# Writing the corner weights ahead of the wait for the transposes, and four value buffers for two, in a deformable convolution's sampling loop

## The chip, the cores and the metric

The kernel runs on one core of one Trainium2 chip (trn2). The metric is the device time of one execution in microseconds. TensorE multiplies and transposes, VectorE and ScalarE work element by element, GpSimd issues the gathers, SyncE issues the plain transfers. Engines run their own instruction streams and meet at semaphores only.

## The reference

Four blocks act on an activation of 8 images of 64 channels and 32x32 pixels, one after the other: attention with a wavelet split, two "adder" convolutions (sums of absolute differences), a quantized pair of 3x3 convolutions, and a residual block with a deformable convolution. The change lies in the last one. Cut to what matters:

```python
h = relu(bn(conv2d(x, rb_w1) + rb_b1, rb_bn1))
h = relu(bn(conv2d(h, rb_w2) + rb_b2, rb_bn2) + x)
off_out = conv2d(h, off_w) + off_b           # 54 maps: 2 groups x 9 taps x (y, x, mask)
py, px = offsets + pixel + tap               # per group, tap, pixel
val = sum over 4 corners of h[corner] * corner weight        # bilinear, zero outside
out = einsum('odck,bdckhw->bohw', dc_w, val * sigmoid(mask)) + dc_b
h = leaky_relu(bn(out, bn1), 0.1)
return x + leaky_relu(bn(conv2d(h, cv2_w), bn2), 0.1)
```

## The kernel before

Two images lie on the 128 partitions at a time (64 channels each), so the eight images are four pairs; "image" below means such a pair, b = 0 to 3. Everything of the earlier blocks is done when the phase `sampler` is at work on its steps.

For each image a chain of seven stages (`stage_pe`, `stage_act`, `stage_dve`, numbered 0 to 6) does the quantized block's convolutions, the two residual convolutions and the offset convolution (nine taps each, into PSUM banks 6 and 7), stores the pixels' channel rows to a table in device memory (each entry holds the four corner pixels of a position), and works out the gather indices `IDX` and the corner weights `W4` (masked, bilinear). For image 0 they run ahead of all steps.

Then an image has 16 steps (`STEPS`), 64 in all: a step `th` is 128 pixels of one of the two images that lie together. Its work is:

1. GpSimd: 18 indirect DMAs, one for each group and tap (line 1902), each fetching 128 table rows of 512 bytes into `G[th % 4]`. It waits for `used`, so a gather buffer is refilled only after its step's reduce, four steps back. These 18 are called a batch below.
2. ScalarE, `weigh(th)` (line 2054): copies the step's 18 x 4 corner weights from `W4` to the single buffer `WP` in PSUM bank 5.
3. VectorE (lines 1951 to 1961): waits for the gathers and the weights, multiplies in place (128 x 2304), reduces over the four corners into `VAL[:, th % 2]`, and frees the gather buffer. In the kernel before it waits ahead of the reduce until the transposes of step th-2 have read that value buffer.
4. TensorE (lines 2003 to 2023): five transposes of the values into PSUM, then, when ScalarE has copied them out, ten matmuls (five products in float32, each sent as two passes) with the kernel weights `DC`. Each is sent with a weight load of its own; the transposes too.
5. ScalarE (lines 2033 to 2047): the copy from PSUM to `VT`, in two instructions.

Eight steps fill a PSUM bank. Then ScalarE copies it to `Y`, VectorE applies the leaky ReLU, TensorE makes the 1x1 convolution (E below), ScalarE copies it to `U`, and VectorE does the last leaky ReLU and the addition (`finish`, lines 1963, 2025, 2056). VectorE's `finish` stands behind the first step of the next bank and waits for all of this.

The order on every engine is written out by `steps` (line 1873): sample step th, at every eighth step `finish` for the bank before, then one stage of the next image. TensorE does stage s behind step s of the 16, ScalarE and VectorE behind step s + 1 (`lag`). So image b + 1 is prepared between the first eight steps of image b; the last image's steps have nothing between them.

T52 and MM52 below are the transposes and the products of step 52.

Of the kernel before, what the change touches and what calls it, by code (L numbers as in the profile page):

```python
# [17 lines left out]
NB = B // HALVES  # L18
# [16 lines left out]
CG = CH // DG  # L35
# [3 lines left out]
STEPS = TILES * HALVES  # L39
GK = DG * TAPS  # L40
# [147 lines left out]
def program(nc, A, C, out):  # L188
# [3 lines left out]
    with outer:  # L192
# [1443 lines left out]
        def sampler(st, sb, sem):  # L1636
# [4 lines left out]


            STAGES = 7
            RING = 4
            ws = ("rb_w1", "rb_w2", "off_w")
            G = [sb(f"G{i}", [128, GK, 4 * CG]) for i in range(RING)]
            VAL = sb("VAL", [128, 2, GK, CG])
            VT = sb("VT", [128, 2, 5, 128])
            Y = sb("Y", [128, 2, BANK])
            U = sb("U", [128, 2, BANK])  # L1650
# [10 lines left out]
                   for i in range(3)]  # L1661
# [15 lines left out]

            arrived = [sem(f"arrived{i}") for i in range(RING)]
            used, val, t_ps, t_sb, d_ps, d_sb, leaky, e_ps, e_sb, final, written = (
                sem(n) for n in ("used", "val", "t_ps", "t_sb", "d_ps", "d_sb", "leaky", "e_ps", "e_sb", "final",  # L1680
                                 "written"))
            valued, weighed = (sem(n) for n in ("valued", "weighed"))
            WP = PS[:, 5, 0:GK * 4]
            off3 = OT[:, :, :].rearrange("p t (h c) -> p (t h) c", h=HALVES)
            PRE = PS[:, 6:8, :]
# [202 lines left out]
            with nc.Block() as blk:  # L1888
# [59 lines left out]
                def _(v):  # L1948
                    def sample(th):
                        gt = G[th % RING]  # L1950
                        v.wait_ge(arrived[th % RING], 16 * GK * (th // RING + 1))
                        v.wait_ge(weighed, th + 1)
                        g3 = gt[:, :, :].rearrange("p k (q c) -> p (k q) c", q=4)
                        v.tensor_tensor(g3, g3, WP.unsqueeze(2).broadcast_to([128, GK * 4, CG]), ALU.mult)  # L1954
                        v.drain()
                        if th >= 2:
                            v.wait_ge(t_ps, th - 1)
                        v.tensor_reduce(VAL[:, th % 2, :, :], gt[:, :, :].rearrange("p k (q c) -> p k c q", q=4),  # L1958
                                        AX.X, ALU.add)
                        v.drain().then_inc(val, 1)  # L1960
                        v.sem_inc(used, 1)
# [39 lines left out]
                @blk.tensor  # L2001
                def _(t):
                    def sample(th):
                        tl, h, k = th // 2, th % 2, th // per_bank
                        t.wait_ge(val, th + 1)
                        if th >= 2:
                            t.wait_ge(t_sb, th - 1)
                        flat = VAL[:, th % 2, :, :].rearrange("p k c -> p (k c)")
                        for c in range(5):
                            n = min(128, GK * CG - 128 * c)  # L2010
                            o = 128 * c if c < 4 else 128 * (th % 2)
                            mm = t.transpose(PS[0:n, th % 2 if c < 4 else 2, o:o + 128],  # L2012
                                             flat[:, 128 * c:128 * c + n], K["ident"][:, :])
                        mm.then_inc(t_ps, 1)
                        t.wait_ge(t_sb, th + 1)
                        if th % per_bank == 0 and k >= 2:
                            t.wait_ge(e_sb, k - 1)
                        for c in range(5):
                            n = min(128, GK * CG - 128 * c)
                            mm = t.matmul(PS[64 * h:64 * h + 64, 3 + k % 2, 128 * (tl % 4):128 * (tl % 4) + 128],  # L2020
                                          DC[0:n, c, :], VT[0:n, th % 2, c, :], start=(c == 0), stop=(c == 4))
                        if th % per_bank == per_bank - 1:
                            mm.then_inc(d_ps, 1)

                    def finish(k):
                        t.wait_ge(leaky, k + 1)
                        t.matmul(bank(3 + k % 2), CV2[:, 0, :], Y[:, k % 2, :], start=True, stop=True)\  # L2027
                            .then_inc(e_ps, 1)
                    steps(t, stage_pe, weights_pe, sample, finish, 0)

                @blk.scalar
                def _(a):
                    def sample(th):
                        k = th // per_bank
                        if th == 0:
                            weigh(0)
                        a.wait_ge(t_ps, th + 1)
                        a.activation(VT[:, th % 2, 0:4, :], PS[:, th % 2, :].rearrange("p (a c) -> p a c", c=128),  # L2038
                                     ACT.Copy)
                        a.activation(VT[0:64, th % 2, 4, :], PS[0:64, 2, 128 * (th % 2):128 * (th % 2) + 128], ACT.Copy)  # L2040
                        a.drain().then_inc(t_sb, 1)  # L2041
                        if th + 1 < NB * STEPS:
                            weigh(th + 1)
                        if th % per_bank == per_bank - 1:
                            a.wait_ge(d_ps, k + 1)
                            a.activation(Y[:, k % 2, :], bank(3 + k % 2), ACT.Identity, scale=INV[:, 2:3],  # L2046
                                         bias=SHIFT[:, 2:3]).then_inc(d_sb, 1)
# [42 lines left out]
```

## Time and profile before

| | |
|---|---|
| median of 3 runs | 4685.74 us (4657.04 to 4686.9) |
| the profiled execution | 4699.3 us, its span 4697.5 us |
| TensorE busy | 3017.8 us (64% of the span) |
| VectorE busy | 2951.6 us (63%) |
| ScalarE busy | 2245.1 us (48%) |
| GpSimd busy | 1156.9 us (25%) |
| packets of the gathers' queue | 36864, 75.57 MB |

Busy time is the time in which an engine executes; waiting for a semaphore isn't in it. In a timeline a row is: start, duration, engine, line of the kernel, operation, what it writes and reads, the count merged, and in brackets how long the engine was idle before it and which engine's event ended that ("issue": nothing that the profile shows; "remote": an event the profile can't place). "PE" is TensorE, "DVE" VectorE, "ACT" ScalarE, "POOL" GpSimd. A matmul's record tells when it was sent to the array and its modelled length; when its result was ready is seen from who waited for it. The two passes of a float32 product have a record each.

### The profile page before, as it was taken

How to read it: one execution, taken by the hardware profiler on the slowest of the kernel's cores; microseconds unless marked ns; L12 is line 12 of the kernel's file. 1: busy time of each engine (PE TensorE's matmuls, PEld its weight loads, DVE VectorE, ACT ScalarE, POOL GpSimd, SP SyncE). 2: the span in 40 equal slices, each digit the busy share in tenths (PEclk: the TensorE clock that was granted, in tenths of full speed). 3: DMA queues.
4: the chain of work that ended last, by engine and by line, in shares of the span. 5: the costliest groups of instructions: out<-in, count | busy, mean ns of one | idle time of the engine just before them, and what ended most of it. 6: DMA issues, size and time to landing. Idle time of an engine off the chain costs nothing. (4 is left out here: it accounts for less than half of the span.)

```text
span 4697.5 us, 54006 instructions
## 1 busy us (share of the span) xinstructions
PE 3017.8 (64%) x20519; PEld 1314.3 (28%) x20519; DVE 2951.6 (63%) x3460; ACT 2245.1 (48%) x1945; POOL 1156.9 (25%) x1229
## 2 busy tenths in 40 slices
PE   3777479999999989999999985143143114411112
PEld 2454333233333333333333332021121112211111
DVE  5999747999999967999999961033321322232222
ACT  1444226999999967999999940000000000000000
POOL 2000010000000000000000002655665665556663
PEclk7665579999999999999999987575566556655555
DMA  2200000000000000000000001112112211211111
GB/s 42 85 1 1 1 3 1 2 1 1 1 2 1 2 1 1 1 1 1 1 2 1 2 13 36 43 42 55 45 49 51 54 47 45 59 40 45 49 44 33
DMA packets 125704, 106.26 MB, mean 23 GB/s; under 512 B 100432, under 2 KB 102608, under 8 KB 125436
## 3 DMA queue, kind: packets, MB, share of 16 engines
q0 software_dynamic: 36864, 75.57, 5.7%
q1 hardware_dynamic: 86940, 26.43, 2.6%
q8 instruction: 184, 3.01, 0.3%
q10 hardware_dynamic: 1632, 0.56, 0.1%
q14 instruction: 84, 0.69, 0.0%
HBM read 82.50 MB, written 19.96 MB: 22 GB/s over the span
## 5 line engine op out<-in xcount | busy, mean ns | idle before, releaser
L1533 ACT ACTIVATE adder_layer_Z<-adder_layer_CP,AN 128x2048 f32 x984 | 1873.9, 2033 | 31.7 <-PE PS L1498 30.9
L1498 PE MATMUL PS<-adder_layer_Z,c_adder_out 128*32 128x512 f32 x16896 | 1843.8, 593 | 57.9 <-ACT adder_layer_Z L1533 33.6
L1579 DVE TENSOR_SCALAR adder_layer_Z<-adder_layer_CP,AW 128x2048 f32 x1128 | 1369.9, 1283 | 43.7 <-PE PS L1498 29.9
L1902 POOL DMA_INDIRECT sampler_G<-neighbours,sampler_IDX x1152 | 1096.5, 952 | 753.5 <-issue 348.3
L1498 PEld LDWEIGHTS PS<-adder_layer_Z,c_adder_out 128*32 128x32 f32 x16896 | 644.5, 110 | 1256.9 <-issue 1187.4
L2038 ACT ACTIVATE sampler_VT<-PS 128x512 f32<-128x512 f32 x64 | 38.2, 598 | 1497.0 <-remote 921.8
L2020 PE MATMUL PS<-sampler_VT,DC 128*64 128x128 f32 (+1 forms) x640 | 157.4, 414 | 897.4 <-ACTq L2041 454.0
L1954 DVE TENSOR_TENSOR sampler_G<-sampler_G,PS 128x2304 f32<-128x2304 f32 x64 | 163.5, 2554 | 840.4 <-issue 436.0
L1586 DVE SCALAR_TENSOR_TENSOR adder_layer_Z<-adder_layer_CP,AW,adder_layer_Z 128x1024 f32<-128x1024 f32 x384 | 476.4, 1282 | 35.6 <-issue 35.6
L2020 PEld LDWEIGHTS PS<-sampler_VT,DC 128*64 128x64 f32 (+1 forms) x640 | 112.9, 210 | 945.5 <-issue 476.0
L2012 PE MATMUL PS<-c_ident,sampler_VAL 128*128 128x128 f32 (+1 forms) x320 | 78.3, 401 | 386.1 <-DVEq L1960 297.3
L1462 POOL MEMSET adder_layer_CP<- 128x4624 f32 x2 | 7.9, 3954 | 1051.0 <-POOLq L1457 1050.8
L1958 DVE TENSOR_REDUCE sampler_VAL<-sampler_G 128x576 f32<-128x2304 f32 x64 | 260.1, 4065 | 5.3 <-issue 0.4
L1467 POOL MEMSET XP<- 128x4624 f32 x1 | 4.0, 3952 | 1045.8 <-PE PS L1512 1045.8
L2012 PEld LDWEIGHTS PS<-c_ident,sampler_VAL 128*128 128x128 f32 (+1 forms) x320 | 52.2, 194 | 420.6 <-DVEq L1960 317.2
L1703 PE MATMUL PS<-XP,WB 128*128 128x512 f32 x288 | 141.8, 656 | 11.5 <-DVEq L1786 5.9
L806 DVE MAX8 top_k_best<-top_k_WK 128x8 f32<-128x256 f32 x384 | 135.1, 415 | 10.3 <-issue 0.5
L694 PE MATMUL PS<-VT,top_k_PT 128*128 128x9 f32 x512 | 102.5, 339 | 50.8 <-ACT top_k_PT L759 50.8
L694 PEld LDWEIGHTS PS<-VT,top_k_PT 128*128 128x128 f32 x512 | 99.5, 298 | 62.2 <-ACT top_k_PT L759 62.2
L744 ACT ACTIVATE top_k_sign<-PS,top_k_nthr 128x256 f32<-128x256 f32 x128 | 59.0, 473 | 107.8 <-DVEq L801 107.8
L1969 DVE SCALAR_TENSOR_TENSOR sampler_U<-sampler_U 128x512 f32<-128x512 f32 x8 | 5.5, 693 | 166.3 <-ACT sampler_U L2058 166.3
L612 POOL TENSOR_TENSOR top_k_after<-top_k_hot,top_k_best 128x96 f32<-128x96 f32 x32 | 12.0, 373 | 383.7 <-DVEq L807 383.7
(342 smaller groups left out, 2082.4 us busy)
## 6 DMA issues: line engine op xcount, KB each, us to landing
sampler_G<-neighbours,sampler_IDX POOLq DMA_INDIRECT x1152
neighbours<-top_k_zero SPq DMA_DIRECT2D x16, 578.0 KB, 7.2
neighbours<-sampler_HT SPq DMA_DIRECT2D x256, 32.0 KB, 1.7
X<-in_x SPq DMA_DIRECT2D x8, 256.0 KB, 6.2
out<-X SPq DMA_DIRECT2D x8, 256.0 KB, 3.1
P<-in_L_conv_conv_w SPq DMA_DIRECT2D x4, 144.0 KB
P<-in_L_conv_add_w SPq DMA_DIRECT2D x4, 144.0 KB
RAW<-in_L_conv_w SPq DMA_DIRECT2D x4, 144.0 KB
```

The lines of the kernel that those rows point to most:

```text
L694: mm = t.matmul(PS[:, 6, D1 * u:D1 * u + D1], PT[:, u, 128 * mt:128 * mt + 128], VTf[:, c:c + D1], start=(mt == 0), stop=(mt == 1))
L806: v.max(best[:, g % 2, u, 8 * r + 1:8 * r + 9], WK[:, u, :])
L1498: mm = t.matmul(PS[32 * j:32 * j + 32, k, :], K["adder_out"][:, 32 * i:32 * i + 32], Z[:, r % SLOTS, j, c:c + BANK], start=False, stop=Fal ...
L1533: op = a.activation(z(r, j), seen(ch, ty, tx), ACT.Relu, bias=ANf[:, weight(ty, tx, j, i)])
L1579: op = v.tensor_scalar(z(r, j), seen(ch, ty, taps[0]), AWf[:, weight(ty, taps[0], j, i)], 0.0, ALU.subtract, ALU.max)
L1586: op = v.scalar_tensor_tensor(out=z(r, j)[:, b], in0=seen(ch, ty, tx)[:, b], scalar=AWf[:, weight(ty, tx, j, i)], in1=z(r, j)[:, b], op0=A ...
L1703: mm = t.matmul(PS[:, 6 + k, :], w[:, tap, :], patch(src, 2 * b + k, tap), start=(tap == 0), stop=(tap == TAPS - 1))
L1902: g.indirect_dma_start(G[th % RING][:, k, :], None, tables[b], bass.IndirectOffsetOnAxis(ap=IDX[:, b % 2, step, k:k + 1], axis=0))\
L1954: v.tensor_tensor(g3, g3, WP.unsqueeze(2).broadcast_to([128, GK * 4, CG]), ALU.mult)
L1958: v.tensor_reduce(VAL[:, th % 2, :, :], gt[:, :, :].rearrange("p k (q c) -> p k c q", q=4), AX.X, ALU.add)
L2012: mm = t.transpose(PS[0:n, th % 2 if c < 4 else 2, o:o + 128], flat[:, 128 * c:128 * c + n], K["ident"][:, :])
L2020: mm = t.matmul(PS[64 * h:64 * h + 64, 3 + k % 2, 128 * (tl % 4):128 * (tl % 4) + 128], DC[0:n, c, :], VT[0:n, th % 2, c, :], start=(c == ...
```

## The change

`VAL` gets four buffers in place of two. A new semaphore, `multiplied`, is raised when VectorE's multiply of a step is done. ScalarE waits for it and writes the next step's weights before it waits for the step's transposes; before, it wrote them after the copy to `VT`. `WP` stays a single buffer. The reduce waits for the transposes four steps back in place of two. Nothing is computed differently.

```diff
-            RING = 4
+            RING, DEPTH = 4, 4
...
-            VAL = sb("VAL", [128, 2, GK, CG])
+            VAL = sb("VAL", [128, DEPTH, GK, CG])
...
-            valued, weighed = (sem(n) for n in ("valued", "weighed"))
+            valued, weighed, multiplied = (sem(n) for n in ("valued", "weighed", "multiplied"))
...
                         v.tensor_tensor(g3, g3, WP.unsqueeze(2).broadcast_to([128, GK * 4, CG]), ALU.mult)
-                        v.drain()
-                        if th >= 2:
-                            v.wait_ge(t_ps, th - 1)
-                        v.tensor_reduce(VAL[:, th % 2, :, :], gt[:, :, :].rearrange("p k (q c) -> p k c q", q=4),
+                        v.drain().then_inc(multiplied, 1)
+                        if th >= DEPTH:
+                            v.wait_ge(t_ps, th - DEPTH + 1)
+                        v.tensor_reduce(VAL[:, th % DEPTH, :, :], gt[:, :, :].rearrange("p k (q c) -> p k c q", q=4),
                                         AX.X, ALU.add)
...
-                        flat = VAL[:, th % 2, :, :].rearrange("p k c -> p (k c)")
+                        flat = VAL[:, th % DEPTH, :, :].rearrange("p k c -> p (k c)")
...
                         if th == 0:
                             weigh(0)
+                        if th + 1 < NB * STEPS:
+                            a.wait_ge(multiplied, th + 1)
+                            weigh(th + 1)
                         a.wait_ge(t_ps, th + 1)
                         a.activation(VT[:, th % 2, 0:4, :], PS[:, th % 2, :].rearrange("p (a c) -> p a c", c=128),
                                      ACT.Copy)
                         a.activation(VT[0:64, th % 2, 4, :], PS[0:64, 2, 128 * (th % 2):128 * (th % 2) + 128], ACT.Copy)
                         a.drain().then_inc(t_sb, 1)
-                        if th + 1 < NB * STEPS:
-                            weigh(th + 1)
```

## Rows read from the trace of the kernel before

**Rows 1.** The page: TensorE's busy tenths in 40 slices of 117 us.
```profile
PE   3777479999999989999999985143143114411112
```

**Rows 2.** Busy time by windows: from the first gather to the end.
```profile
2894.80:4697.50 1802.70, 491.82 (x1510) 272.21 (x1510) 496.40 (x242) 92.12 (x225) 1096.44 (x1152) 0.57 0.18 47
```

**Rows 3.** Groups by line, 2890 to 4697 us: busy, mean ns; idle before, by releaser.
```profile
L1902 POOL DMA_INDIRECT sampler_G<-neighbours,sampler_IDX x1152 | 1096.5, 952 | 753.5 <-issue 348.3 <-DVEq L1961 302.2 <-DMA neighbours<-sampler_HT 102.9
L1958 DVE TENSOR_REDUCE sampler_VAL<-sampler_G 128x576 f32<-128x2304 f32 x64 | 260.1, 4065 | 5.3 <-issue 0.4
L1954 DVE TENSOR_TENSOR sampler_G<-sampler_G,PS 128x2304 f32<-128x2304 f32 x64 | 163.5, 2554 | 840.4 <-issue 436.0 <-ACT PS L2054 362.1 <-DMA sampler_G<-neighbours,sampler_IDX 42.2
...
L2038 ACT ACTIVATE sampler_VT<-PS 128x512 f32<-128x512 f32 x64 | 38.2, 598 | 1497.0 <-remote 921.8 <-issue 369.0 <-PE PS L2012 206.1
...
L2054 ACT ACTIVATE PS<-sampler_W 128x72 f32<-128x72 f32 x64 | 15.0, 234 | 14.6 <-DVEq L1833 8.3
```

**Rows 4.** Timeline of TensorE, steps 53 and 54: start, duration, idle before.
```profile
4447.30 1.33 PE L2012 MATMUL PS<-c_ident,sampler_VAL 128*128 128x128 f32 x5 [4.55 <-issue]
4482.17 2.58 PE L2020 MATMUL PS<-sampler_VT,DC 128*64 128x128 f32 x10 [33.54 <-issue]
4489.30 1.33 PE L2012 MATMUL PS<-c_ident,sampler_VAL 128*128 128x128 f32 x5 [4.55 <-DVEq L1960]
```

**Rows 5.** Timeline of VectorE, the reduces of steps 54 and 55.
```profile
4485.17 4.05 DVE L1958 TENSOR_REDUCE sampler_VAL<-sampler_G 128x576 f32<-128x2304 f32 x1
...
4525.09 4.05 DVE L1958 TENSOR_REDUCE sampler_VAL<-sampler_G 128x576 f32<-128x2304 f32 x1
```

**Rows 6.** Timeline of ScalarE, the copies to VT of steps 53 to 56.
```profile
4481.34 0.60 ACT L2038 ACTIVATE sampler_VT<-PS 128x512 f32<-128x512 f32 x1 [40.91 <-remote]
...
4521.27 0.60 ACT L2038 ACTIVATE sampler_VT<-PS 128x512 f32<-128x512 f32 x1 [38.84 <-remote]
...
4530.60 0.60 ACT L2038 ACTIVATE sampler_VT<-PS 128x512 f32<-128x512 f32 x1 [8.24 <-PE PS L2012]
...
4539.93 0.60 ACT L2038 ACTIVATE sampler_VT<-PS 128x512 f32<-128x512 f32 x1 [5.11 <-issue]
```

**Rows 7.** Timeline of TensorE: products of step 15; a convolution.
```profile
3401.22 2.59 PE L2020 MATMUL PS<-sampler_VT,DC 128*64 128x128 f32 x10 [5.83 <-ACTq L2041]
...
3462.02 1.01 PE L1703 MATMUL PS<-XP,W 128*128 128x512 f32 x1 [2.21 <-issue]
```

**Rows 8.** Timeline of ScalarE: copy of a bank to Y; copy of step 16.
```profile
3427.03 0.78 ACT L2046 ACTIVATE sampler_Y<-PS,SHIFT,INV 128x512 f32<-128x512 f32 x1 [25.55 <-remote]
3441.03 0.60 ACT L2038 ACTIVATE sampler_VT<-PS 128x512 f32<-128x512 f32 x1 [13.22 <-remote]
```

**Rows 9.** Timeline of GpSimd: gathers around a pause.
```profile
4509.62 0.94 POOL L1902 DMA_INDIRECT sampler_G<-neighbours,sampler_IDX  x1 [0.30 <-issue]
4510.87 0.95 POOL L1902 DMA_INDIRECT sampler_G<-neighbours,sampler_IDX  x1 [0.30 <-issue]
4529.54 0.94 POOL L1902 DMA_INDIRECT sampler_G<-neighbours,sampler_IDX  x1 [17.73 <-DVEq L1961]
```

**Rows 10.** Timeline at step 4: convolution of the next image, and batch 8.
```profile
3107.95 17.70 PE L1703 MATMUL PS<-P,WB 128*128 128x512 f32 x36
...
3112.94 0.95 POOL L1902 DMA_INDIRECT sampler_G<-neighbours,sampler_IDX  x1 [9.86 <-DVEq L1961]
```

**Rows 11.** Granted clock (after the instructions of five engines): a slow and a clear stretch.
```profile
4440.00:4481.00 41.00, 3.91 (x15) 2.73 (x15) 6.61 (x2) 0.33 (x2) 30.94 (x34) 0.50 0.19 53
4522.00:4541.00 19.00, 8.07 (x31) 5.70 (x32) 13.91 (x5) 2.99 (x9) 8.72 (x10) 0.50 0.10 29
```

**Rows 12.** Timeline of the end: copy of step 63, last product, last addition.
```profile
4683.89 0.60 ACT L2038 ACTIVATE sampler_VT<-PS 128x512 f32<-128x512 f32 x1 [8.24 <-PE PS L2012]
...
4688.92 2.08 PE L2027 MATMUL PS<-sampler_Y,CV 128*128 128x512 f32 x2 [1.62 <-DVEq L1967]
...
4692.62 0.69 DVE L1971 TENSOR_TENSOR X<-X,sampler_U 128x512 f32<-128x512 f32 x1
```

## The prediction

> **What bounds the kernel now.** The page's forty slices of TensorE come first [rows 1]. Up to about 2,890 us TensorE is nearly full; that is the work of earlier layers, which the change doesn't touch. From there on it is at one to four tenths. The stretch from 2894.8 us has 1802.7 us, 1096 of them busy on GpSimd, 492 on TensorE [rows 2]. Next the cost groups give one operation each of the 64 steps: 18 gathers of 0.952 us, a multiply of 2.554, a reduce of 4.065, the copy to VT of 0.598, the weights of 0.234 [rows 3]; five transposes take 1.33, ten products 2.58 [rows 4]. A gather starts 1.25 us after the last [rows 9], so a step is worth 22.5 us of GpSimd and 64 steps 1440; VectorE needs 6.7. Some 360 us of the 1803 are thus not gathers.
>
> The idle time in the same groups says where these sit: ScalarE's copy waits 921.8 + 369.0 + 206.1 us for the transposes, VectorE's multiply 436.0 + 362.1 us for the weights, GpSimd 302.2 us for a free gather buffer [rows 3]. It is one chain: ScalarE writes the weights of step th+1 only behind its copy of step th, the copy waits for TensorE, and the multiply waits for the weights.
>
> Then I asked why the transposes are late. In the steps 53 and 54 TensorE sends the products of a step, 4.6 us later the transposes of the next, and before the products it stood still for 33.5 us [rows 4]; ScalarE's copy runs at 4481.34 and 4521.27, 33 and 31 us behind the end of the transposes' records [rows 6]. Where the products' own end can be seen, at the eighth step of a bank, they took as long: sent at 3401.22, their copy ran at 3427.03 (25.8 us), and the next transposes' at 3441.03, 14.0 us later [rows 7, 8]. Ten products are 20 instructions with their weight loads, five transposes 10: 1.3 to 1.4 us for each, whatever its size, 40 us a step. A convolution shows the same from the sending side: late in it a load and a matmul take 2.8 us (idle 2.21 and 0.59 of the matmul before) [rows 7]. So while gathers are issued TensorE works off a backlog at some 0.75 instructions per us. It isn't always so: the copies at 4530.60 and 4539.93 come 9.33 us apart [rows 6], just behind a pause of GpSimd of 17.73 us [rows 9], and a convolution of 72 instructions takes 17.7 us, begun in a pause of 9.86 us and 12.7 us into the next gathers [rows 10]. I call these slow and clear spells: a clear one begins at the latest some 9 us after the last gather (4511.8 to 4521.3 [rows 6, 9]) and outlasts the restart by 10 to 20 us. The clock isn't it: a slow and a clear stretch both show 0.50, the 1.2 GHz level [rows 11].
>
> **The change part by part.** (a) Order on ScalarE. The weights of th+1 (0.234 us) are now written after the multiply of th and ahead of the wait for the transposes of th. 64 new waits on the multiply are added; behind each stand the copy to VT and through it all of TensorE's products. But the transposes that the copy waits for come a 4.05 us reduce after that multiply, so the new wait always ends first: cost 0, at most 64 reads of a semaphore, under 0.1 us each by the 0.08 us from the reduce's end at 4489.22 to the transposes at 4489.30 [rows 4, 5]. The new increment rides on a drain that is there: 0. Should the weights write delay the copy, that is 0.3 us a step, 19 us in all as the upper bound; the lower one is a gain, 2.6 us a step (c). I take 0 for the write itself, since ScalarE is idle between multiply and transposes: its copies waited 8 to 41 us [rows 6].
>
> (b) Four value buffers. The reduce of th no longer waits for the transposes of th-2 but of th-4. That wait was never the last one (idle ahead of the reduces is 5.3 us over 64 [rows 3]); cost and gain 0. What it allows is used by (a) alone, and (a) allows one step: the weights of th+2 still stand behind the copy of th. So VectorE gets one step further ahead of TensorE.
>
> (c) Clear steps. Now the loop is multiply, reduce, transposes, copy, weights: 9.33 us. Then it is VectorE's 6.7 alone: 2.6 us less for each step that is neither slow nor gather-bound. In the middle this buys nothing, since GpSimd has restarted with the first buffer. At the end, when the gathers are over, it counts.
>
> (d) Slow steps. TensorE does 30 instructions at 1.33 whoever waits; the transposes already stand in its queue. What moves is the release of the gather buffer, by one step of 40 us. I replay the last image. The multiply of each step takes the place of the one before it, so the reduce of step 55 ends at 4489.2 in place of 4529.1 [rows 5], and the pause of 17.73 us vanishes: batch 59 starts at 4509.7, batch 60 at 4532.2, 20 us sooner than before (4529.54 + 22.5 = 4552.0). But step 56 ends a bank: VectorE's `finish` waits for TensorE's last product of it (E), behind MM54, T55, MM55, T56, MM56 and E, 84 instructions, and with the pause TensorE has lost its clear spell. GpSimd runs dry at 4554.7, TensorE is clear at 4564, the rest of the chain takes 19.4 us (copy 0.9, products 2.6, transposes 1.3, copy 0.9, products 2.6, from E to the last addition 4.4 [rows 12], step 57's 6.7), and batch 61 starts at 4583.5, against 4574.6: 9 us later. The last gather ends at 4651 in place of 4642. TensorE is then a step further (T61 at 4660), and T62 and T63 follow at some 5 each: the last copy at 4670.5 in place of 4683.89 [rows 12], the end 13 us sooner.
>
> (e) The three images with convolutions between steps. VectorE is held to TensorE anyway at steps 1 and 7 of 16 (stages 0 and 6 wait for ScalarE behind the copy) and by `finish` at steps 0 and 8. Each pause saved in between is paid back there, as in (d): I take 0 for them, between -18 (one pause of 17.7 kept) and +25 (below) each.
>
> Sum: -13. The profiled execution took 4699.3 us (span 4697.5) and gives 4686; it lies 13.6 above the median shown, 4685.7, which gives 4673. The three runs span 30 us, so about 1% (47 us) is what a measurement can tell from no change.
>
> **The rivals.** *Pauses saved and not paid back.* For it: GpSimd's 302.2 us all end with a release that comes a step sooner. Against it: the replay, where TensorE lives from these pauses. One pause of 17.7 in each of four images, and the tail: -83, 4603.
>
> *Slower: the convolution loses its clear spell.* At step 4 of each image GpSimd pauses 9.86 us; the products and a convolution, 92 instructions, then take some 21 us [rows 10]. With the multiply of step 4 no longer behind the copy of step 3, batch 8 follows without a pause, and these 92 go at 1.33: after 22.5 + 9 us, when GpSimd has run dry, 24 are done, and the rest needs 15: 46 us in place of 21, +25 in each of three images, with the tail +62: 4748. It decides if no pause falls just ahead of this convolution; where one comes anyway, it is nothing.
>
> *The spells are the chain's, not TensorE's.* If the transposes were late only through the order of waits, all 360 us would go: 1440 + 14 behind 2894.8, about 4350. Against it stand the 25.8 us of the products [rows 7, 8], in front of which nothing waits. The Trainium skill ("SBUF — State Buffer", Who interferes with whom) has it that TensorE never waits on another engine's use of the memory and that a DMA slows no compute engine; by that rule this case would hold. The trace speaks against the rule, or for a path that isn't the memory's.
>
> *It does nothing*, each wait moving to the next: 4686, inside my forecast.
>
> **How the numbers follow.** Forecast, with its own range of 4645 to 4710: 0.55. Pauses kept (4603 to 4645): 0.26. Slower (4725 to 4750): 0.15. The chain's: 0.04. Faster by over 1% (under 4639): most of 0.26, 0.04, and a little of the forecast: 0.31. Slower (over 4733): 0.15 and 0.01 of the forecast: 0.16. Within: 0.53. The range of 4600 to 4728 leaves out the fourth case and most of the third.
>
> **What the changed profile would show.** The weights' write before the copy in each step; in slow stretches a multiply and reduce on the place of the step before, and copies still 40 us apart. GpSimd's waits fewer but longer, their sum near 300. At the end copies 5 to 7 us apart in place of 9.33. If copies in the slow stretches come closer than 40 us, I am wrong toward faster; if the convolution of step 4 takes 40 us, the slower rival holds.

## The result, and the profile after

The changed kernel takes 4729.52 us (median of 6 runs, 4706.85 to 4743.53) against 4682.31 (6 runs, 4657.04 to 4687.32): a ratio of 1.0102 [1.0072, 1.0133], 47 us slower. The forecast was 4673, its range 4600 to 4728: the result lies just outside it, on the slow side. The profiled execution took 4730.5 us, its span 4728.7.

TensorE's forty slices come first, on the page of the changed kernel, then its windows from the first gather to the end.

```profile
PE   3777479999999989999999974241044104410203
```

```profile
2890.50:4728.70 1838.20, 480.38 (x1510) 268.96 (x1510) 496.81 (x242) 91.68 (x225) 1094.06 (x1152) 0.58 0.17 46
```

Up to 2890 us nothing changed [rows 1]. The sampling stretch is 35.5 us longer, 1838.2 for 1802.7, with the same instructions and nearly the same busy times on every engine [rows 2]. So all of it is waiting, and the groups by line tell whose (busy, mean ns; idle before, by releaser):

```profile
L1902 POOL DMA_INDIRECT sampler_G<-neighbours,sampler_IDX x1152 | 1094.1, 950 | 816.4 <-DVEq L1961 366.2 <-issue 346.1 <-DMA neighbours<-sampler_HT 104.2
L1958 DVE TENSOR_REDUCE sampler_VAL<-sampler_G 128x576 f32<-128x2304 f32 x64 | 260.7, 4074 | 7.9 <-issue 0.5
L1954 DVE TENSOR_TENSOR sampler_G<-sampler_G,PS 128x2304 f32<-128x2304 f32 x64 | 163.5, 2554 | 643.3 <-issue 424.3 <-ACT PS L2055 171.9 <-DMA sampler_G<-neighbours,sampler_IDX 47.0
...
L2041 ACT ACTIVATE sampler_VT<-PS 128x512 f32<-128x512 f32 x64 | 38.2, 597 | 1527.7 <-remote 1268.4 <-PE PS L2012 168.4 <-issue 90.9
L2055 ACT ACTIVATE PS<-sampler_W 128x72 f32<-128x72 f32 x63 | 14.7, 233 | 162.9 <-DVEq L1955 97.9 <-issue 63.0
```

The change does what it says: VectorE's multiply waits 172 us for the weights where it waited 362, and the weights' write now waits for the multiply (97.9 us). But the first row is the one that sets the end: GpSimd waits 366.2 us for a free gather buffer in place of 302.2 [rows 3]. The gathers' own 1440 us are the same in both, so the 35.5 us are these pauses and the tail. Pauses of GpSimd over 0.9 us: 16 with 366.2 us in all, before 21 with 306.0, so +60; from the end of the last gather to the end of the span 31.8 us (4696.8 to 4728.7), before 55.7 (4641.8 to 4697.5), so -24; together 36.

By image, from its first gather to the next image's: 443.1, 477.6, 456.0 and (to the last gather's end) 429.6 us; before 441.5, 449.6, 442.1 and 413.8. That is +1.6, +28, +14 and +16. These are single executions; how the extra time is spread over the images changes from one to the next (experiment 1).

In the slow stretches the copies are as far apart as before [rows 6]; at the end they are closer than the 9.33 us of before [rows 12]. ScalarE's timeline of the changed kernel, and the last product and addition:

```profile
4428.28 0.60 ACT L2041 ACTIVATE sampler_VT<-PS 128x512 f32<-128x512 f32 x1 [23.89 <-issue]
4470.28 0.60 ACT L2041 ACTIVATE sampler_VT<-PS 128x512 f32<-128x512 f32 x1 [40.91 <-remote]
4512.31 0.60 ACT L2041 ACTIVATE sampler_VT<-PS 128x512 f32<-128x512 f32 x1 [40.94 <-remote]
...
4705.68 0.60 ACT L2041 ACTIVATE sampler_VT<-PS 128x512 f32<-128x512 f32 x1 [14.37 <-remote]
4710.38 0.60 ACT L2041 ACTIVATE sampler_VT<-PS 128x512 f32<-128x512 f32 x1 [3.62 <-PE PS L2012]
4715.09 0.60 ACT L2041 ACTIVATE sampler_VT<-PS 128x512 f32<-128x512 f32 x1 [3.95 <-PE PS L2012]
...
4720.12 2.07 PE L2027 MATMUL PS<-sampler_Y,CV 128*128 128x512 f32 x2 [1.62 <-DVEq L1967]
...
4723.82 0.69 DVE L1971 TENSOR_TENSOR X<-X,sampler_U 128x512 f32<-128x512 f32 x1
```

**Where the time goes.** I took the start of each of the 64 copies to `VT` and compared the distances, step by step. Many places change by tens of us up or down; one change repeats in all three images with convolutions. From the copy of step 5 to that of step 6 it is 73.4, 72.1 and 72.2 us, before 23.3, 26.8 and 23.0. The step ahead of it is shorter, 10.7, 10.7 and 11.2 for 37.4, 37.4 and 37.7, so the pair, copy 4 to copy 6, takes 84.1, 82.8 and 83.3 in place of 60.6, 64.2 and 60.6: some 22 us more each. Between these two copies TensorE has the offset convolution (stage 5, line 1703, 36 matmuls), which stands behind step 5. The timeline of the changed kernel at that place of image 1 (steps 19 to 23 of all):

```profile
3588.35 0.60 ACT L2041 ACTIVATE sampler_VT<-PS 128x512 f32<-128x512 f32 x1 [70.64 <-remote]
3591.69 16.28 PE L1703 MATMUL PS<-P,WB 128*128 128x512 f32 x36
3608.55 0.60 ACT L2041 ACTIVATE sampler_VT<-PS 128x512 f32<-128x512 f32 x1 [18.02 <-PE PS L2012]
3613.76 4.05 DVE L1958 TENSOR_REDUCE sampler_VAL<-sampler_G 128x576 f32<-128x2304 f32 x1
3618.21 0.95 POOL L1902 DMA_INDIRECT sampler_G<-neighbours,sampler_IDX  x1 [40.62 <-DVEq L1961]
3619.26 0.60 ACT L2041 ACTIVATE sampler_VT<-PS 128x512 f32<-128x512 f32 x1 [5.32 <-PE PS L2012]
3620.77 4.11 DVE L1958 TENSOR_REDUCE sampler_VAL<-sampler_G 128x576 f32<-128x2304 f32 x1
3622.61 16.18 PE L1703 MATMUL PS<-XP,WB 128*128 128x512 f32 x36
3627.83 4.13 DVE L1958 TENSOR_REDUCE sampler_VAL<-sampler_G 128x576 f32<-128x2304 f32 x1
3638.63 0.71 PE L2012 MATMUL PS<-c_ident,sampler_VAL 128*128 128x128 f32 x5
...
3684.50 0.95 POOL L1902 DMA_INDIRECT sampler_G<-neighbours,sampler_IDX  x1 [0.31 <-issue]
3691.34 0.60 ACT L2041 ACTIVATE sampler_VT<-PS 128x512 f32<-128x512 f32 x1 [70.02 <-remote]
...
3720.25 1.33 POOL L1902 DMA_INDIRECT sampler_G<-neighbours,sampler_IDX  x1 [34.80 <-DVEq L1961]
```

And the kernel before at the same place:

```profile
3617.55 0.60 ACT L2038 ACTIVATE sampler_VT<-PS 128x512 f32<-128x512 f32 x1 [36.31 <-remote]
...
3620.89 17.23 PE L1703 MATMUL PS<-XP,WB 128*128 128x512 f32 x36
3625.87 0.95 POOL L1902 DMA_INDIRECT sampler_G<-neighbours,sampler_IDX  x1 [13.83 <-DVEq L1961]
3637.95 0.71 PE L2012 MATMUL PS<-c_ident,sampler_VAL 128*128 128x128 f32 x5
3644.37 0.60 ACT L2038 ACTIVATE sampler_VT<-PS 128x512 f32<-128x512 f32 x1 [24.80 <-remote]
...
3652.66 0.95 POOL L1902 DMA_INDIRECT sampler_G<-neighbours,sampler_IDX  x1 [4.58 <-DVEq L1961]
```

Before, the convolution is sent 5 us ahead of a batch that had waited 13.83 us, one buffer is free, and 22.5 us later GpSimd waits again. After, three reduces follow each other at 3613.8, 3620.8 and 3627.8, since the weights no longer wait for the copies: three buffers come free before the convolution's results, and GpSimd issues 54 gathers without a pause from 3618.2 to 3685.5. Both convolutions were sent in 16 to 17 us. But the transposes behind it, sent at 3638.63, were ready for the copy at 3691.34, 5.9 us after the last of the 54 gathers. Copy, products and with them `finish` waited that long, and then GpSimd waited 34.8 us.

That pair is not yet the whole account. The two distances behind it are shorter than before, 28.0, 30.0 and 28.8 us for 59.4, 32.9 and 60.0, since the kernel before has a slow step there in two of the three images (35.9 and 36.5 us from copy 6 to copy 7). From copy 4 to copy 8 the three images take 337.1 us, before 337.8. Beside the kernel before, the extra time shows from copy 1 to copy 4 (319.7 for 273.0) and from copy 8 to the first copy of the next image (642.7 for 599.4), with 31.6 less from copy 0 to copy 1. In the other execution with this order on ScalarE (experiment 1) only the second of these is as large: 288.3, 640.4, and 10.4 more from copy 0 to copy 1. Why the last eight steps take longer is not shown. What the late convolution costs must be read beside a kernel whose weights are early elsewhere; experiment 2 has it.

The rival's place is in the same rows: the convolution behind step 3 of the image, sent at 3591.69. There the copies are 20.2 us apart (3588.35 to 3608.55), as before (21.7): here the pause, of 40.62 us, came just ahead of and over it. In the other images 23.6 and 39.3 (before 21.6 and 20.7).

### The profile page after: what moved, and what is told of

Read it like the earlier page. It is cut to its first block and busy times, and to the rows that moved or that the text cites. A ratio compares the mean times of both kernels' runs of the same rounds, so it can differ in the third digit from the quotient of the medians.

```text
span 4728.7 us, 54009 instructions
## 1 busy us (share of the span) xinstructions
PE 3001.3 (63%) x20519; PEld 1308.7 (28%) x20519; DVE 2952.1 (62%) x3460; ACT 2244.9 (47%) x1945; POOL 1154.5 (24%) x1229
## 5 line engine op out<-in xcount | busy, mean ns | idle before, releaser
L1533 ACT ACTIVATE adder_layer_Z<-adder_layer_CP,AN 128x2048 f32 x984 | 1873.9, 2015 | 31.6 <-PE PS L1498 30.8
L1902 POOL DMA_INDIRECT sampler_G<-neighbours,sampler_IDX x1152 | 1094.1, 950 | 816.4 <-DVEq L1961 366.2
```

Of the source, the lines that this page charges most:

```text
L1533: op = a.activation(z(r, j), seen(ch, ty, tx), ACT.Relu, bias=ANf[:, weight(ty, tx, j, i)])
L1902: g.indirect_dma_start(G[th % RING][:, k, :], None, tables[b], bass.IndirectOffsetOnAxis(ap=IDX[:, b % 2, step, k:k + 1], axis=0))\
```

## The experiments

Every ratio is to runs of the kernel before on the same chip. Two kinds of chip turned up: on three chips the kernel before took 4671 to 4685 us, on two others 4364 to 4366, with the same instructions. No chip of the experiments came twice, so whether it is the chip itself or something around it at that time is open; "chip" below means the one or the other. The runs of the latter kind are told further down, with what they mean. Distances between copies are of one execution each.

**1. Which part.** The order alone, with two value buffers, and the four buffers alone, with the weights behind the copy:

```diff
-            RING, DEPTH = 4, 4
+            RING, DEPTH = 4, 2      # first run: changed kernel with two buffers
...
+                        early = False   # second run: four buffers, weights behind the copy
-                        if th + 1 < NB * STEPS:
+                        if th + 1 < NB * STEPS and early:
                             a.wait_ge(multiplied, th + 1)
                             weigh(th + 1)
...
+                        if th + 1 < NB * STEPS and not early:
+                            weigh(th + 1)
```

> The change with two value buffers as before; only the weights' order is changed. Theory (the order alone lets VectorE run one step ahead, the two more buffers are never used): within 0.3% of the changed kernel, so 1.007 to 1.013 of the kernel before; the copy of step 6 comes some 72 us after that of step 5 in each of the first three images. Rival (the deeper value buffer lets the gathers run away): about 1.000, and that interval stays near 24 us.

4732.75 us (8 runs), 1.0097 [1.0064, 1.0130]; copy 5 to copy 6: 72.7, 72.1, 72.0 us. By its trace the three images with convolutions are 31 us longer than before, where the changed kernel's are 43.5: so much do two executions of the same order differ.

> Four value buffers and the new increment, but the weights are written behind the copy as before. Theory: no wait was ended by this, so 0.998 to 1.002 of the kernel before. Rival (the deeper buffer is the cause): 1.007 to 1.013.

4684.38 us (12 runs), 1.0001 [0.9979, 1.0023]. The whole effect is ScalarE's order; two of the four value buffers are never needed.

**2. Which steps.** The weights early in some steps only, behind the copy in the others; the four runs differ in one line.

```diff
+                        early = th >= 3 * STEPS                                  # last image
+                        early = th >= 3 * STEPS or th % STEPS >= 8               # steps without a stage
+                        early = th >= 3 * STEPS or th % STEPS not in (4, 5, 6)   # all but three
+                        early = th < 3 * STEPS and th % STEPS in (4, 5, 6)       # these three alone
```

> Weights ahead only in the last 16 steps, where no convolution stands between steps. Theory (the loss is made at the convolutions): the first three images as before, the last one 8 to 13 us shorter, ratio about 0.998. Rival (being a step ahead costs in the plain steps too, by fewer pauses of GpSimd): the last image no shorter or longer, 1.000 to 1.004.

4676.32 us (12 runs), 0.9979 [0.9958, 1.0001], 8.5 us, as the theory had it; the interval just reaches no change. The last copies are 4.7 us apart.

> Weights ahead in steps 8 to 15 of each image and in all of the last; behind the copy in steps 0 to 7 of the first three, where the convolutions stand. Theory: the 72 us between the copies of steps 5 and 6 are back to some 24 us, ratio 0.990 to 1.000. Rival (the loss is made in the plain steps): 1.005 to 1.010.

4656.74 us (12 runs), 0.9946 [0.9919, 0.9972]. The time is in the theory's band; the interval from copy 5 to 6 is 26.1, 49.8 and 49.7 us, not 24 each. So early weights gain where no convolution of the next image stands between the steps, and the loss of the changed kernel is made in the first eight steps of an image. This version beats both kernels. Without a change of operands it is the fastest, level with the next one.

> Weights early everywhere except behind steps 4, 5 and 6 of the first three images, where they stand behind the copy as before. If the whole loss is made by the three buffers released in a row at steps 5 to 7, ahead of the offset convolution: the copy interval from step 5 to 6 is back at 20 to 27 us in place of 72, and the time is that of the kernel with early weights in the plain steps alone, 0.990 to 0.998. If the earlier releases of steps 0 to 3 and 7 cost as well (as holding the gathers left 1.0033): 1.002 to 1.007. On a chip that shows no slow steps: 1.000, and nothing is told.

4652.72 us (12 runs; before 4670.91), 0.9969 [0.9954, 0.9984]. The time fell into the band of the first theory; my figure for the interval from copy 5 to 6 did not, it was 49.5 us in each image. The step ahead of it was 10.5 to 10.7, and the pair, copy 4 to copy 6, is 60.1, 60.2 and 60.0, as before. I had named one interval of two that trade time; the table below has the sums.

> The counterpart: weights early behind steps 4, 5 and 6 of the first three images alone. If these three steps carry the loss: 1.008 to 1.014 (three intervals of 72 us in place of 24, partly given back, and no gain in the plain steps). If the loss needs the early releases of the steps before them too: 1.000 to 1.005. On a chip that shows no slow steps: 1.000.

4693.52 us (7 runs), 1.0056 [1.0036, 1.0076], between the two bands. Copy 4 to copy 6 is 83.6, 89.0 and 83.0: the convolution is as late as in the changed kernel. GpSimd's waits in the groups of these two kernels, first with these three steps behind the copy, then with these three alone early:

```profile
L1902 POOL DMA_INDIRECT sampler_G<-neighbours,sampler_IDX x1152 | 1093.1, 949 | 726.8 <-issue 345.1 <-DVEq L1961 277.6 <-DMA neighbours<-sampler_HT 104.2
```

```profile
L1902 POOL DMA_INDIRECT sampler_G<-neighbours,sampler_IDX x1152 | 1093.8, 949 | 775.2 <-issue 347.7 <-DVEq L1961 323.5 <-DMA neighbours<-sampler_HT 104.0
```

The distances around the offset convolution, in us, for the three images that have one:

| kernel | copy 4 to 6 | copy 6 to 8 | copy 4 to 8, summed |
|---|---|---|---|
| before | 60.6, 64.2, 60.6 | 59.4, 32.9, 60.0 | 337.8 |
| the changed kernel | 84.1, 82.8, 83.3 | 28.0, 30.0, 28.8 | 337.1 |
| early in the plain steps | 63.3, 60.9, 59.1 | 33.0, 33.0, 33.0 | 282.3 |
| behind the copy at steps 4 to 6 | 60.1, 60.2, 60.0 | 33.0, 33.0, 33.0 | 279.2 |
| early at steps 4 to 6 alone | 83.6, 89.0, 83.0 | 28.8, 28.4, 28.8 | 341.6 |

Where the other steps are early, early weights at steps 4 to 6 thus cost 58 us here (279.2 to 337.1), some 19 an image; by the ratios it is 62 in all.

Beside each other the runs give a square. Early weights at these three steps cost 0.56% alone, and 1.33% (0.9969 to 1.0102) when all other steps are early too. All other steps together gain 0.31%, the plain ones alone 0.54%; whether the difference, the cost of steps 0 to 3 and 7, is real these intervals don't tell. Three steps of 16 make the loss, and more than half of it only together with the others. The table suggests why, though no run tries it apart: the kernel before loses time from copy 6 to copy 7 in two of three images anyway, so there the late convolution takes the place of another loss, while beside early weights elsewhere (9.4 us at that place) it comes on top.

**3. The gathers held back at the offset convolution.** The changed kernel, but GpSimd starts the batch that would run over it only when the convolution is done.

```diff
                         if th >= RING:
                             g.wait_ge(used, th - RING + 1)
+                        if step == 9 and b + 1 < NB:
+                            g.wait_ge(off_ps, b + 2)
```

> The change with GpSimd held until the next image's offset convolution is done. If slow spells show here (the kernel before near 4680): 0.990 to 1.000 of the kernel before, the copies of steps 5 and 6 some 20 us apart in place of 72; rival, the gathers are innocent and only GpSimd's time counts: 1.010 to 1.025. Without spells: 1.000 to 1.001.

4694.89 us (12 runs; before 4679.61), 1.0033 [1.0009, 1.0057], outside both bands. Copy 5 to copy 6 went from 72 to 21.1, 20.5 and 20.7 us, so it is the gathers over the convolution that make it late. But they are not had for nothing:

```profile
L1904 POOL DMA_INDIRECT sampler_G<-neighbours,sampler_IDX x1152 | 1098.3, 953 | 760.9 <-issue 349.1 <-DVEq L1963 159.2 <-PE PS L1703 148.4
```

The hold itself is 148.4 us of GpSimd's waiting (pauses of 43, 42 and 64 us), and all its waits for buffers and the hold sum to 307.6, where the changed kernel had 366.2. From copy 4 to copy 8 the three images take 186.8 us, where the changed kernel has 337.1, but from copy 8 to the next image's first copy 770.3 where it has 642.7; copy 2 to copy 3, ahead of the hold, is 56.7, 46.1 and 83.7 for 54.5, 71.7 and 24.0. Some 0.7% of the 1.0% came back.

**4. What a slow step is made of.** The products' operands in bf16 (`VT` and `DC` are rounded to it), in the kernel before: a product is then one pass, and a step 20 TensorE instructions in place of 30.

```diff
-        DC = l3("DC", [128, 5, CH])
+        DC = l3("DC", [128, 5, CH], BF16)
-            VT = sb("VT", [128, 2, 5, 128])
+            VT = sb("VT", [128, 2, 5, 128], BF16)
```

> The kernel before with products in bfloat16, 10 instructions in place of 20. With slow spells: 0.955 to 0.975 and slow copies 27 us apart in place of 40 (rival, a fixed wait for a group: 0.990 to 1.000 and 40 us). Without: 1.000.

4617.93 us (4 runs; before 4679.61), 0.9861 [0.9821, 0.9901]. ScalarE's timeline, in the plain steps of image 2 and from there on:

```profile
4309.55 0.60 ACT L2038 ACTIVATE sampler_VT<-PS 128x512 bf16<-128x512 f32 x1 [13.47 <-remote]
4337.55 0.60 ACT L2038 ACTIVATE sampler_VT<-PS 128x512 bf16<-128x512 f32 x1 [26.91 <-issue]
4365.55 0.60 ACT L2038 ACTIVATE sampler_VT<-PS 128x512 bf16<-128x512 f32 x1 [26.91 <-issue]
```

28.0 us a step: 1.40 us for each of 20 instructions, against 42 us for 30. The price per instruction holds. The gain in time was less than expected, between the two bands. As I read it, at 28.0 us a step there are fewer pauses (16 for 21) and so fewer clear spells: the last four distances of each of the first three images are 28.0 now. No run tries this apart.

The two edits that gained, together (early weights in the plain steps, bf16 products):

> Early weights in the plain steps alone, and the products' operands in bf16 (VT and DC are rounded to bf16, so each product is one pass and not two: 20 TensorE instructions a step in place of 30). The two singly gave 0.9946 and 0.9861. If their gains are of separate steps they add: 0.978 to 0.983. If both live from the same slow steps of the last eight of an image, most of one is lost: 0.984 to 0.988. On a chip that shows no slow steps: 0.9997.

4621.55 us (6 runs; before 4670.91), 0.9900 [0.9877, 0.9922]. Neither band: beside bf16 the early weights bring nothing that shows, 0.9900 against 0.9861, with intervals that overlap.

**5. Which transfers.** The kernel before, GpSimd issuing plain transfers of the same size in place of the indirect ones. They read fixed rows, so this kernel leaves out the sampling at the offsets; it tells of time only:

```diff
-                            g.indirect_dma_start(G[th % RING][:, k, :], None, tables[b],
-                                                 bass.IndirectOffsetOnAxis(ap=IDX[:, b % 2, step, k:k + 1], axis=0))\
+                            g.dma_start(G[th % RING][:, k, :], tables[b][128 * k:128 * k + 128, :])\
```

> The kernel before with the indirect DMAs replaced by plain ones of the same size, fixed rows, issued by GpSimd as before; the output is not the reference's. With slow spells on this chip: if DMAs that GpSimd issues are what slows TensorE, slow copies stay 40 us apart; if the indirect form is, they vanish. Without spells: the time is that of GpSimd's issuing, 4366 if a plain DMA takes its 1.25 us too, under 4200 if it takes less.

3742.23 us (2 runs; before 4679.61), 0.7994 [0.7955, 0.8034]. Its groups, the gathers and the copy to `VT`:

```profile
L1902 POOL DMA_DIRECT2D sampler_G<-neighbours x1152 | 612.9, 541 | 295.9 <-DVEq L1960 182.8 <-DMA neighbours<-sampler_HT 103.5 <-issue 9.6
...
L2037 ACT ACTIVATE sampler_VT<-PS 128x512 f32<-128x512 f32 x64 | 38.2, 597 | 693.0 <-PE PS L2011 693.0
```

An issue takes 541 ns in place of 952, and the copy's waits all end with the transposes themselves, none as "remote": no step is slow, on a chip where the kernel before has its slow steps. The same bytes in the same count, moved at twice the rate (100 GB/s over the sampling stretch, the changed kernel 46), don't make TensorE late; the indirect form does, or the scattered rows that come with it (the plain transfers read rows in order, and the two were not tried apart). The same transfers issued by SyncE (with the next image's stores put in at step 12):

> The kernel before with the 18 indirect DMAs of a step replaced by 18 plain ones of the same 128 rows of 512 bytes, fixed rows, issued by SyncE; GpSimd issues none. The output is not the reference's. Theory A (issuing from GpSimd makes TensorE late): no slow spells, copies 9.4 us apart or at the pace of the issuing, TensorE's copies never over 1 us late in steps without a convolution, ratio under 0.92. Theory B (the traffic into SBUF or the DMAs' completions do it): slow spells of 1.3 us an instruction stay.

3753.88 us (2 runs; before 4366.39), 0.8597 [0.8581, 0.8612]. This one was on a chip without slow steps, so it tells of the gathers' issue alone: it is what bounds the kernel there.

**6. The chips without slow steps.** Eight runs fell on two such chips. What was expected of those not told so far (the three steps, the held gathers and bf16, twice each, and the changed kernel once more):

> Weights ahead everywhere but in steps 4, 5 and 6 of the first three images (so the multiplies of steps 5 to 7 stay behind the copies). Theory (the loss is made there, as the steps 5 to 7 release three gather buffers at once just ahead of the offset convolution): interval of the copies of steps 5 and 6 near 24 us, ratio 0.990 to 0.998. Rival (it is made at every convolution, at steps 1 to 3 too): 1.000 to 1.006.

> The change, and GpSimd waits ahead of batch 9 of each of the first three images until the next image's offset convolution is done: gathers are delayed on purpose. Theory (gathers that are issued make TensorE's results late, so holding them pays): the interval of the copies of steps 5 and 6 falls from 72 to some 20 us, ratio 0.990 to 1.000 of the kernel before, where the change alone has 1.010. Rival (the gathers are innocent, GpSimd's time is what counts): 1.010 to 1.025.

> The kernel before with VT and DC in bfloat16: the products of a step are five matmuls with one pass each, 10 instructions in place of 20, on rounded operands. Theory (in a slow spell each TensorE instruction costs 1.33 us whatever its size): copies in slow stretches 27 us apart in place of 40, ratio 0.955 to 0.975. Rival (what is slow is a fixed wait for each group of instructions, or the reading of the values): the interval stays near 40 us, 0.990 to 1.000.

> The changed kernel again, as the anchor of this group, since in the last group the kernel before took 4366 us and no run showed a slow spell. Theory (the change acts only through the slow spells, and these come and go with the chip or its surroundings): 1.007 to 1.013 if the kernel before takes some 4680 here; 0.998 to 1.001 if it takes some 4366, with gathers without pauses. Rival (the change has a cost of its own): above 1.005 in both.

> The change with GpSimd held until the next image's offset convolution is done, again. If the kernel before takes some 4680: 0.990 to 1.000, the copies of steps 5 and 6 some 20 us apart in place of 72 (rival, gathers are innocent: 1.010 to 1.025). If it takes some 4366: 1.000 to 1.002.

> The kernel before with VT and DC in bfloat16, so the products are 10 instructions in place of 20, on rounded operands. If the kernel before takes some 4680: 0.955 to 0.975, slow copies 27 us apart in place of 40 (rival, a fixed wait for a group: 0.990 to 1.000 and 40 us). If some 4366: 1.000.

> Weights ahead everywhere but in steps 4, 5 and 6 of the first three images, again. If the kernel before takes some 4680: 0.990 to 0.998, the copies of steps 5 and 6 near 24 us apart (rival, the loss is made at every convolution: 1.000 to 1.006). If some 4366: 1.000.

| kernel | time, us | ratio |
|---|---|---|
| before, two chips | 4366.39; 4364.02 | |
| the changed kernel | 4365.11 | 1.0002 [0.9992, 1.0011] |
| behind the copy at steps 4 to 6 | 4368.77; 4364.89 | 1.0004 [0.9995, 1.0013]; 1.0002 [0.9993, 1.0011] |
| gathers held | 4367.18; 4366.95 | 1.0001 [0.9992, 1.0010]; 1.0006 [0.9997, 1.0015] |
| bf16 products | 4366.13; 4363.04 | 0.9998 [0.9989, 1.0007]; 0.9997 [0.9987, 1.0006] |

Where no step is slow, these runs tell no theory of slow steps from another. What they show is what is left of each edit without them: nothing that shows. The changed kernel on such a chip, its page's slices and its groups:

```profile
POOL 2000000000000000000000000037777777777775
```

```profile
L1902 POOL DMA_INDIRECT sampler_G<-neighbours,sampler_IDX x1152 | 1096.0, 951 | 455.1 <-issue 350.8 <-DMA neighbours<-sampler_HT 104.3
L1954 DVE TENSOR_TENSOR sampler_G<-sampler_G,PS 128x2304 f32<-128x2304 f32 x64 | 163.4, 2554 | 871.5 <-DMA sampler_G<-neighbours,sampler_IDX 871.0 <-issue 0.6
L2041 ACT ACTIVATE sampler_VT<-PS 128x512 f32<-128x512 f32 x64 | 38.2, 597 | 353.9 <-PE PS L2012 353.9
```

GpSimd never waits for a buffer, the multiply waits for gathers alone (871.0 us) and never for the weights, and the copy for the transposes' own end. The wait that the change removes doesn't exist there. A step there is the gathers' 22.5 us, at the end as in the middle.

## Why the prediction was wrong

**(a) and (b), right.** Cost and gain 0 for the write itself and for the buffers: four buffers alone 1.0001, the order with two buffers the same as with four, and the whole change 1.0002 where no step is slow. (The copies' waits in [rows 6] go down to 5.11 us, not to 8; the sum doesn't use it.)

**(c), right.** The slow steps kept their 40 to 42 us; the last copies came 4.7 us apart, below the 5 to 7 named, since VectorE's 6.7 us had already been done and only copy, products and transposes were left.

**(d), right in kind.** I had the last gather of the last image 9 us later and the tail 22 us shorter. Measured: its gathers take 16 us more, the tail 24 less. Early weights in the last image alone gave -8.5 us in place of -13, with an interval that just reaches 0.

**(e), the step that failed:** "Each pause saved in between is paid back there, as in (d): I take 0 for them". The payment was taken to be as large as the saving. Measured, the three images are 43.5 us longer (1.6 + 28 + 14), +14.5 each: inside the ends of -18 and +25 given for it, but not 0, and this one term carried the sign. (The second execution of this order, with two value buffers, has +31 for the three.) With (d) at -8 and a first gather 4.3 us sooner it makes the 31 us by which the profiled execution is longer, where -13 was forecast. The runs split it in two of opposite sign. The last eight steps of these images gain some 20 us (4676.32 to 4656.74, experiment 2). The first eight lose over three times that (0.9946 to 1.0102, 73 us), nearly all by the releases at steps 4 to 6 (0.9969 to 1.0102, 62 us).

**The slower rival had the mechanism and the wrong place.** A convolution loses the pause that it ran in: some 22 us from copy 4 to copy 6 in each of three images, and 19 up to copy 8 beside a kernel that is early elsewhere, near the rival's +25. But it named the convolution of step 4, where in the changed kernel nothing moved in two of three images, because a pause came there anyway, which was the rival's own condition. Where none came the rival's place was hit too: with the weights behind the copy at steps 4 to 6 it is the copies around this first convolution that are 39.5, 33.8 and 38.8 us apart (before 21.6, 21.7 and 20.7). I had not asked the same of the second convolution, behind step 5, though the kernel before has a pause of 13.83 us there too. What made it the place in the changed kernel, as I read the rows, is that VectorE is held to TensorE at steps 1 and 7 and by `finish` at 0 and 8, and runs free in between: there its releases come three in a row. The question for each of the convolutions was how many buffers are free ahead of it, not whether one pause vanishes. The chance of 0.15 was too small for a mechanism with a price of +25 in three places.

**The rivals that were faster.** "Pauses saved and not paid back" is refuted by the sum of the waits, 366 for 302. "The spells are the chain's" is refuted where there are spells, since with the chain cut the copies stay 42 us apart. Its time of 4350, though, is that of the chips without them (4364 to 4366): 64 steps at the gathers' own distance.

**The signs named.** Copies in slow stretches 40 us apart: seen. Waits fewer but longer, sum near 300: fewer and longer (16 for 21), but the sum is 366; this sign was the one to tell (e) wrong. The convolution of step 4 at 40 us: in one image of three (39.3).

## What to carry to other kernels

Where one engine's issue slows another, buffers that come free earlier are not free of charge: look at what the slowed engine has in its queue at that moment, and release early only where it is short. Here that is early weights in the steps with no convolution between them (0.9946), not in all (1.0102). A replay of one stretch doesn't price the others: replay each place at which a long job stands in the slowed queue. And a time that differs by 7% from one chip's runs to another's, as this kernel's does, is to be taken on both kinds before an edit is judged. Last, an interval that grows is a cost only if the ones behind it don't shrink: sum up to a place where both kernels are in step again.

## What the runs showed of the hardware

**The slow steps come with some chips and with the indirect transfers.** In the experiments three of five chips ran the kernel before in 4671 to 4685 us, two in 4364 to 4366. On the former, while GpSimd issues indirect transfers (but for the first 10 to 20 us behind a pause), TensorE's completions come at some 1.33 to 1.40 us per instruction, weight loads counted: 42 us for the 30 of a step, 28.0 for 20. With plain transfers from the same engine they don't. The granted clock in the sampling stretch is the same on both kinds (0.58 and 0.59), so it isn't the clock. Why some chips do it stays open, and so does the path. Every execution here carries the profiler's span and clock and none is there without them, so it is not shown either whether the recording of the instructions has a part in it. The Trainium skill ("SBUF — State Buffer", Who interferes with whom) has it that a transfer never contends with a compute engine. The plain transfers and the two quicker chips agree; the three chips with indirect ones don't, and there the measurement decides as to the effect. Whether it is the memory's ports that they meet at, no run shows.

**What is late is the end that others see.** In the kernel before, ten products, the E of step 15 and a convolution are sent one behind the other. Timelines of TensorE and ScalarE, then the windows:

```profile
3444.37 2.08 PE L2027 MATMUL PS<-sampler_Y,CV 128*128 128x512 f32 x2
...
3446.24 11.01 PE L1703 MATMUL PS<-XP,W 128*128 128x512 f32 x25
...
3472.53 0.78 ACT L2058 ACTIVATE sampler_U<-PS,SHIFT,INV 128x512 f32<-128x512 f32 x1 [30.42 <-remote]
```

```profile
3427.00:3446.00 19.00, 4.14 (x12) 2.69 (x13) 0.69 (x1) 1.76 (x4) 14.42 (x16) 0.50 0.18 52
3446.00:3460.00 14.00, 11.84 (x27) 4.84 (x25) 0.00 (x0) 0.00 (x0) 10.65 (x12) 0.98 0.19 52
```

E was sent at 3444.37, and 25 matmuls behind it within 14 us, at a granted clock of 0.98 (the 2.4 GHz level); ScalarE saw E's result at 3472.53, 26 us after its modelled end. I had priced a convolution over gathers as sent and done at 1.33 us an instruction. In the changed kernel's rows above it is sent in 16 us, as in a pause; at other places the sending slows late in it, to one matmul in 2.80 us [rows 7]. In either case, who waits for it, or for anything behind it, is late: 52.0 us from the transposes' modelled end at 3639.3 to the copy at 3691.34.
